# Attention 0: the scores of the unit two on ahead of the transposes of this one

## The reference

```
x = _rmsnorm(hidden_states, ln_w)
q = jnp.einsum('bqd,hd->bqh', x, wq).reshape(B, Qlen, N_HEADS, HEAD_DIM)
k = jnp.einsum('bkd,hd->bkh', encoder_hidden_states, wk).reshape(B, Klen, N_KV_HEADS, HEAD_DIM)
v = jnp.einsum('bkd,hd->bkh', encoder_hidden_states, wv).reshape(B, Klen, N_KV_HEADS, HEAD_DIM)
...
scores = jnp.einsum('bhqd,bhkd->bhqk', q, k) / np.sqrt(HEAD_DIM).astype(np.float32)
attn = jax.nn.softmax(scores.astype(jnp.float32), axis=-1).astype(q.dtype)
out = jnp.einsum('bhqk,bhkd->bhqd', attn, v)
```

## Time and profile before

| What | us |
|---|---|
| Median of 3 runs | 1483.76 (1482.83 to 1484.01) |
| The profiled execution | 1481.44 |
| Its span, first to last instruction | 1479.70 |
| Attention 0, the units of all batches | 182 to 681 |

### The profile page before, as it was taken

How to read it: one execution, slowest core, us unless ns; L and a number is a source line. 1 busy time by engine, 2 the same in 40 slices (tenths; PEclk the granted TensorE clock), 3 DMA queues, 4 the chain that set the end, 5 groups by cost and what they waited for, 6 DMA issues and landing times. The chain is left out here.

```text
span 1479.7 us, 28536 instructions
## 1 busy us (share of the span) xinstructions
PE 1370.6 (93%) x10775; PEld 1116.3 (75%) x10783; DVE 971.7 (66%) x1566; ACT 745.7 (50%) x1881; POOL 425.5 (29%) x472
## 2 busy tenths in 40 slices
PE   6998799999999999987999999999779999999488
PEld 6998788989889898855888888888556666666244
DVE  4353387766767777665232356668557999998797
ACT  4231177676767767763111110113157777777396
POOL 0010001101011010010110222332268888888423
PEclk9999899999999999998999999999889999999889
DMA  6742555552544536464445452202342222221023
GB/s 226 247 151 85 97 139 132 133 137 73 150 119 127 148 81 176 120 198 158 160 169 199 153 199 104 72 28 73 103 111 65 65 65 65 64 64 44 1 86 143
DMA packets 127910, 174.93 MB, mean 118 GB/s; under 512 B 27799, under 2 KB 96919, under 8 KB 127792
## 3 DMA queue, kind: packets, MB, share of 16 engines
q1 hardware_dynamic: 127792, 173.26, 40.4%
HBM read 86.94 MB, written 35.29 MB: 83 GB/s over the span
## 5 line engine op out<-in xcount | busy, mean ns | idle before, releaser
L1151 ACT ACTIVATE a_prob<-a_psS,a_negmax 128x256 f32<-128x256 f32 x512 | 236.8, 483 | 153.0 <-DVE a_negmax L1063 152.6
L1063 DVE TENSOR_REDUCE a_negmax<-a_psS 128x4 f32<-128x1024 f32 x128 | 154.3, 1206 | 69.1 <-PE a_psS L956 67.4
L881 POOL COPY a_recip<-a_recip_head 128x256 f32<-128x256 f32 x64 | 25.6, 400 | 519.6 <-DVE a_recip_head L1114 519.6
L931 PE MATMUL a_psQ<-a_xT_hi,wide 128*128 128x256 f32 x912 | 170.6, 288 | 1.1 <-DVE a_q_lo L1058 0.7
L1378 PE MATMUL m_psY<-wide,m_a_hi 128*128 128x512 f32 x512 | 159.9, 394 | 6.8 <-DVE m_a_lo L1426 6.8
L1378 PE MATMUL m_psY<-w_ffn,m_a_hi 128*128 128x512 f32 x512 | 158.3, 390 | 0.0
L966 PE MATMUL a_psT<-ident,a_prob 128*128 128x128 f32 x1024 | 137.3, 278 | 14.0 <-issue 6.0
L931 PEld LDWEIGHTS a_psQ<-a_xT_hi,wide 128*128 128x128 f32 x912 | 138.6, 189 | 9.9 <-issue 5.8
L966 PEld LDWEIGHTS a_psT<-ident,a_prob 128*128 128x128 f32 x1024 | 116.4, 143 | 23.4 <-issue 13.3
L1168 ACT COPY a_probT<-a_psT 128x512 f32<-128x512 f32 x208 | 115.7, 609 | 35.5 <-PE a_psT L966 34.3
L931 PE MATMUL a_psQ<-a_xT_lo,wide 128*128 128x256 f32 x456 | 127.4, 279 | 0.0
(11 more groups left out here) (236 smaller groups left out, 3002.5 us busy)
## 6 DMA issues: line engine op xcount, KB each, us to landing
a_q_stack<-a_q_hi SPq DMA_DIRECT2D x128, 128.0 KB, 2.7
a_q_stack<-a_q_lo SPq DMA_DIRECT2D x128, 128.0 KB, 2.6
c_raw<-lay_ctxT SPq DMA_DIRECT2D x16, 512.0 KB, 5.0
rows<-in_x SPq DMA_DIRECT2D x8, 1024.0 KB, 6.2
scratch_o<-a_oT SPq DMA_DIRECT2D x16, 512.0 KB, 3.0
m_x<-in_x SPq DMA_DIRECT2D x8, 1024.0 KB, 5.9
scratch_x<-m_x SPq DMA_DIRECT2D x8, 1024.0 KB, 5.1
b_q_stack<-b_q_hi SPq DMA_DIRECT2D x64, 128.0 KB, 2.3
```

What stands on the lines that cost most here:

```text
L881: nc.gpsimd.tensor_copy(recip[:, t % 2], recip_head[:, t % 2].unsqueeze(3).broadcast_to([P, TT, JH0, HD0])).then_inc(recip_ready, 1)
L931: last = nc.tensor.matmul(bank[:, 0:S], w[:, kt, t * P:(t + 1) * P], a[:, kt, :], start=(kt == 0 and w is wq.hi and a is xT_hi), stop=(kt ...
L1063: nc.vector.tensor_reduce(negmax[:, n % 2, :], psS[:, bank:bank + 2, :].rearrange("p a (j k) -> p (a j) k", k=S), AX_X, ALU.max, negate=Tr ...
L1151: last = nc.scalar.activation(prob[:, n % 2, j, :], psS[:, 2 * (n % 2) + j // 2, (j % 2) * S:(j % 2 + 1) * S], ACT.Exp, bias=negmax[:, n % ...
```

## The change

In PE's loop over the units the scores of unit n + 2 come ahead of the transposes of unit n. The wait for the exponentials of unit n, which was the first line of `transposes`, moves out of it and stands at the head of the unit, ahead of both. The other engines' programs stay as they are, and no instruction is added or left out.

```
             def transposes(b, n):
-                pe.wait_ge(exp_done, UNITS * b + n + 1)
                 for kt in range(TT):
                     pe.wait_ge(psT_copied[kt], UNITS * b + n + 1)
...
                     for n in range(UNITS):
-                        transposes(b, n)
+                        pe.wait_ge(exp_done, UNITS * b + n + 1)
                         if n + 2 < UNITS:
                             scores(b, i, u, n + 2)
                         elif more:
                             scores(b + 1, i + u, 1 - u, n + 2 - UNITS)
+                        transposes(b, n)
                         if n:
                             values(b, u, n - 1)
```

## The result

The changed kernel takes 1479.66 us, the median of 20 executions, against 1483.67 for the kernel before, also of 20 (one execution of each, 2747 and 1980 us, was disturbed and does not count in the ratio). The ratio is 0.9969, 95% interval 0.996 to 0.9977: 0.31% faster, 4.6 us. (The ratio goes by the means, 1478.9 and 1483.5; the medians are 4.0 us apart.) The forecast was 1480.2, 3.6 us less than before, so the sign and nearly the size were right. The profiled execution has a span of 1477.8 us (before 1479.70), so only 1.9 us of the gain are seen in this pair of profiles.

A forecast was written before the change was run, and what follows sets the result against it. PE was taken to bound the kernel, busy 93% of the span. Gaps in units 0 to 4 (-1.9, -0.7) and DVE's queue (-1.0), with the rest 0, took 1483.76 by -3.6 to 1480.2 us; range 1477 to 1487.

The forecast's parts named there:

- The packed unit: Units where PE never waits: both orders take equally long, 0 give or take 0.03 us for each of 119 units.
- Rival (a): Switching costs: each transpose group behind scores loses up to 0.08 us, +5.9 us in all, so 1489.7; chance 0.12.
- Units 0 to 4 with the wait: Batches 1, 3, 5, 6: scores fill PE's wait for ACT's copy ahead of unit 2's transposes, gaining 4 x 0.48 = 1.9 us.
- Rival (b): Lead given back: ACT or DVE paces the next transposes, or half the gains meet another wait; about 1482, chance 0.30.
- Batches 0, 2 and 4: Scores fill a gap ahead of unit 4's transposes, gaining about 0.23 us each, 0.7 us in three batches.
- DVE's queue: Earlier scores let DVE's maximum end before its evacuation, shortening the query's waits for DVE's split: 1.0 us gained.
- The cover: Odd units from 5 on: transposes 0.49 us later delay DVE's copy, but 3.5 us cover this; cost 0, uncovered 20.
- The last batch: Early lead 0.65 us lost at unit 6, where scores await stacking DMAs; faster maxima return 0.3: 0, from -0.65 to +0.5.
- The sum: All terms over the kernel: -1.9 - 0.7 - 1.0 + 0 = -3.6 us, giving 1480.2 us.
- Rival (c): Nothing changes: PE's work is the same and gaps only move from before transposes to before values; 1483.8, chance 0.08.
- Rival (d): Stacking DMAs land behind scores at unit 6 or 14 in other batches, 1 us in each of 7; 1487.2, chance 0.05.

The follow-up runs named there:

- experiment 6: The changed kernel with PE's loop over batch pairs written out and scores also waiting for the previous unit's first copy; 1478.36 us, 0.9966 to the kernel before.
- the second half alone: Against the changed kernel: scores ahead of transposes only from unit 5 on, old order in units 0 to 4; 1485.08 us, ratio 1.001 to the kernel before.
- experiment 5: Against the changed kernel: from unit 5 on the previous unit's values also go ahead of the transposes; 1479.16 us, ratio 0.9974 to the kernel before.
- e6: The changed kernel with PE's loop over pairs of batches written out, other engines' loops kept; 1472.05 us, ratio 0.9927 to the kernel before.
- e6 again: The changed kernel with only PE's loop over batch pairs written out, run once more in a second set; 1473.18 us, ratio 0.993 to the kernel before.
- e7: The kernel before, in its old order, with PE's loop over pairs of batches written out; 1479.05 us, ratio 0.9968 to the kernel before.
- the first half alone: Against the changed kernel: scores ahead of transposes only in units 0 to 4, old order from unit 5 on; 1476.54 us, ratio 0.9964 to the kernel before.
- experiments 1: The changed kernel run once more without any edit, beside the kernel before; 1481.63 us, ratio 0.9979.
- 3: Against the changed kernel: scores stay first but wait for the previous unit's first copy, as transposes did before; 1480.29 us, ratio 0.998 to the kernel before.

## Why the prediction was right, step by step

**The packed unit, 0 give or take 0.03: right.** 1.67 against 1.66 us, and 3.50 from S to S. Rival (a), 0.08 lost at each of 119 switches, would have made it 3.58. The single row on which it rested, 0.57 us from S to T in the earlier trace rows, was the copy's, as read: behind S in a packed unit T comes after 0.48.

**Units 0 to 4 with the wait, 4 x 0.48: right.** V(1) leads by 0.49, 0.49, 0.50 and 0.49 in batches 1, 3, 5 and 6. The wait put back takes these away (V(1) at -0.04 or -0.05). Rival (b), the lead given back, falls by the first table: the leads of 0.5 are all still there at unit 15, because PE is busy for the rest of the batch.

**Batches 0, 2 and 4, 3 x 0.23: right in two, mis-sized in one.** 2 and 4 gain 0.26 each, batch 0 gains 0.48. That batch was wrongly put with the others. Its gap stands ahead of T(2), not T(4), and its gain stays when the wait is put back (0.48 at V(4) in experiment 6's kernel as well). The traces show why. Before (ACT's copies of unit 1, then T(2)):

```profile
188.15 1.08 ACT L1168 COPY a_probT<-a_psT 128x512 f32<-128x512 f32 x2
188.86 0.86 PEld L966 LDWEIGHTS a_psT<-ident,a_prob 128*128 128x128 f32 x8 [0.33 <-issue]
```

After (V(0) of the batch comes at 187.54 before and 189.20 after):

```profile
189.02 1.09 ACT L1168 COPY a_probT<-a_psT 128x512 f32<-128x512 f32 x2
190.65 0.90 PEld L965 LDWEIGHTS a_psT<-ident,a_prob 128*128 128x128 f32 x8
```

T(2) started 0.11 us behind the end of the first copy (188.15 + 0.60), its distance in batch 3 too, which points to this copy as what held it. The copy began 0.61 us behind V(0). In the new order it begins 0.18 ahead of V(0), with the wait put back 0.32 ahead, and nothing waits for it. At n = 0 PE has stood for 3 us, and S(2) now starts as soon as the exponentials are there instead of 1.55 us later behind a T at the low clock. The maximum, the exponentials of unit 2 and the copy behind them all follow sooner. So 0.30 of the 0.48 is a second way in which the order gains: the chain behind S starts earlier. No experiment takes it apart from the rest.

**DVE's queue, 1.0: right.** The six waits of 0.33 and the one of 1.01 lost 6 x 0.13 and 0.20, 1.0 us. Between V(4) and V(15) the leads grow by a little more, 0.12, 0.12, 0.20, 0.29, 0.12, 0.19 and 0.17, 1.2 us in all; the second half alone gives 0.83 in its five batches. The chain of batch 6 came as told, maximum before O and the wait from 1.01 to 0.81.

**The cover, 0: right**, by experiment 5, which found 0.3 us a batch for a shift larger than the change's.

**The last batch, 0 from -0.65 to +0.5: right, but for the way back.** The lead by V(4) is 0.44 and not 0.65, S(8) waits 0.62 to 0.66 us for the landing where about 0.8 was forecast, and V(5) comes 0.27 later than before where 0.3 was forecast. What failed is the step behind it: the faster maxima did not give that back in units 8 to 12. The batch ends 0.26 later than before, and 0.4 to 1.1 later in the written-out kernels (e6 and e6 again against e7).

**The sum.** Measured inside the batches: 2.0 + 1.0 + 1.2 - 0.3 = 3.9 us against 3.6 forecast. The times say 4.6 and 3.1, both intervals hold 3.9 (0.26% of 1483.7, a ratio of 0.9974), and at equal clock it is 3.0 give or take 0.6. That the median of the result came within 0.6 us of the forecast is partly luck: the parts that the clock and the rest of the program move from one execution to the next are as large as the gain.

**Rival (c)** falls with the packed rows above. By the Trainium skill (Perfetto Trace Analysis, Identifying Performance Opportunities) the gain would have to come from improving the most-contended engine, picked by occupancy; here that engine's busy time went up by 2.8 us and the kernel is 0.31% faster, so read as a rule on work alone it missed this change. **Rival (d)**: no wait ahead of S at n = 14 is seen, and the second table has no batch of 0 to 6 with its -1 us there.

**What stays open.** What the last 0.18 us of batch 0 are; whether the first half alone beats the whole; and how the order of the program and the clock's falls hang together, since the gain at equal clock (3.0) is smaller than the plain one of the result (4.6).

## What to carry to other kernels

When an engine runs groups in a fixed order, ask of each stop which later group already had all it needs: that group moved ahead is worth the shorter of the stop and its own length (0.49 of a stop of 0.71 here, 0.26 of one of 0.25), and nothing directly where the engine is packed; there it can only shorten the chains that start behind it. Price each stop separately, by the lead that remains at a later steady mark, for here the sum of such small terms repeated better than the medians did. And look at what the moved group itself waits for in every batch: here one of 128 units, whose landing had been covered by the group that now stands behind it, took back a good tenth of the gain.

## What the runs showed of the hardware

**At a loop's turn PE stands for some 3.1 us.** PE's weight loads at the second iteration, before:

```profile
308.47 0.86 PEld L966 LDWEIGHTS a_psT<-ident,a_prob 128*128 128x128 f32 x8 [3.13 <-issue]
```

After:

```profile
308.92 0.93 PEld L956 LDWEIGHTS a_psS<-a_k_stack,a_q_stack 128*128 128x128 f32 x4 [3.14 <-issue]
```

And in the changed kernel with PE's loop written out, at the same place:

```profile
305.94 0.42 PEld L915 LDWEIGHTS a_psQ<-ident,rows 128*128 128x128 f32 x4 [0.94 <-issue]
```

The stop waits for no semaphore that the profile shows, and both loop ends have it. Without the loop, in the old order, the batches across the two boundaries are 3.80 and 4.05 us shorter and the ones behind them 0.65 longer, so a turn costs 3.2 to 3.4 us. Of the 3.80 the stop is 3.1 - 0.9 = 2.2; the other 1.6 goes with the lower clock after it, 0.88 over the 14 us against 1.00. The 0.65 is given back because T(2) now waits for the copy in batches 2 and 4 as well, where the stop had hidden this: the four waits of the earlier trace rows are six in that kernel.

What the stop does go with is a packet of the instruction queue. PE's 3.12 us without a load at the first turn, DMA in 305.35 to 308.47 us:

```profile
q8 instruction: 1, 0.02, 2.2%
```

It holds 16 KB, starts at 305.70 and takes 1.1 us. The stop is 2.8 to 3.5 us long in the traces with the loop, and in all of them such a packet starts 0.3 to 0.9 us into it; in the written-out kernels none starts between 304 and 313 us, and there are 81 in all instead of 86. It ends well before PE goes on, so that it is the cause of the whole stop is not shown. The Trainium skill (Advanced Engine Details and Errata, Control Flow Timing) gives some 0.05 to 0.11 us for a branch; a loop's turn is not that cheap in this trace.

**The clock after a stop comes out two ways.** The table by windows (granted clock is the third figure from the end) of the kernel before:

```profile
140.00:160.00 20.00, 12.41 (x79) 11.64 (x78) 7.70 (x14) 0.00 (x0) 0.00 (x0) 0.83 0.35 86
304.00:318.00 14.00, 11.08 (x113) 9.71 (x112) 8.76 (x15) 8.93 (x33) 0.40 (x1) 0.88 0.59 153
...
640.00:670.00 30.00, 25.71 (x238) 16.81 (x236) 18.82 (x30) 18.63 (x66) 4.42 (x7) 0.94 0.54 182
```

Of the changed kernel:

```profile
140.00:160.00 20.00, 12.42 (x66) 11.60 (x66) 6.85 (x12) 0.00 (x0) 0.00 (x0) 0.66 0.35 86
304.00:318.00 14.00, 11.09 (x104) 9.81 (x102) 7.71 (x13) 8.48 (x30) 0.40 (x1) 0.76 0.58 151
```

Of units 0 to 4 alone:

```profile
304.00:318.00 14.00, 11.20 (x138) 9.58 (x131) 11.18 (x19) 10.23 (x37) 0.80 (x2) 1.00 0.61 158
...
640.00:670.00 30.00, 26.02 (x248) 17.19 (x246) 18.03 (x27) 17.77 (x62) 4.16 (x6) 1.00 0.50 161
```

Of the change with PE's loop written out:

```profile
304.00:318.00 14.00, 13.15 (x153) 11.12 (x152) 13.63 (x22) 12.36 (x44) 0.81 (x2) 1.00 0.68 177
```

All but the last stand for 2.9 to 3.1 us inside 304 to 318. Afterwards TensorE was granted 0.88, 0.76 or 1.00 of full speed over the 14 us, that is, it spent 3.4, 6.7 or 0 of the 14 us at 1.2 GHz and the others at 2.4 (worked out from the mean: 2 x 0.12 and 2 x 0.24 of the window). Units 0 to 4 alone got the full 1.00 there, and its batch 1 gains 2.19 us where the change loses 0.48. In the last batch PE waits 2.9 us for DVE ahead of unit 10, at 655 to 658 us; the executions with 1.00 in 640 to 670 (experiments 1, both halves, 3 and the written-out one with the wait) gain 1.6 to 1.7 us at that one unit, and those with 0.94 gain 0.3 or less there. The same six matmuls behind that stop, in the two executions of the changed kernel, show what it is made of:

```profile
656.14 2.78 PE L1005 MATMUL a_psQ<-a_q_hi,a_wsum 128*40 128x256 f32 x6 [2.50 <-DVE a_update L1095]
```

and at full clock:

```profile
657.21 1.49 PE L1005 MATMUL a_psQ<-a_q_hi,a_wsum 128*40 128x256 f32 x6 [2.50 <-DVE a_update L1095]
```

The stop ahead of them is the same 2.50 us in both. The two traces of the one changed kernel differ in this (0.94 and 1.00 there, 0.88 and 0.76 in 429 to 443), so it is not a property of the program alone. Together with the unsteady parts ahead and behind it makes the times scatter: the kernel before lies within 1481.7 to 1486.3, the changed one within 1474.0 to 1483.2. In the profile pair of the result this works against the change by 1.7 us ahead of attention 0 (0.66 against 0.83 in 140 to 160 us; V(0) of batch 0 comes at 189.20 and not at 187.54) and about 1.1 us at the first boundary, which is why the spans differ by 1.9 us only (0.4 comes from behind attention 0). What decides between the outcomes was not tried.
